# The expert stage of a five-stage kernel: blocks of 288 tokens with both layers' weights stationary

## The reference

```python
probs = softmax(ln(t) @ gate_w.T)          # 8 experts
top_v, top_i = top_k(probs, 2)
for e in range(8):
    h = silu(ln(t) @ w1[e] + b1[e])        # 512 -> 2048
    y = h @ w2[e] + b2[e]                  # 2048 -> 512
    out += y * comb_w[..., e:e+1]          # zero where e is not among the token's two
```

## Time and profile before

| what | value |
|---|---|
| three runs | 1467.91, 1471.44, 1472.68 us, median 1471.44 |
| the profiled execution | span 1469.3 us, mean granted clock 0.912 |
| expert stage, ahead of the loop | 931.5 to 986.05 us |
| its loop | 986.05 us to the last matmul at 1455.25 us |
| after the last matmul | to 1469.3 us |
| PE / DVE / ACT / POOL busy | 84% / 69% / 52% / 20% of the span |

### The profile page before, as it was taken

One profiled execution on the slowest core, in us unless ns is written; L12 is line 12 of the kernel. 1 busy time (PEld: TensorE's weight loads), 2 busy tenths in 40 slices (PEclk: granted clock), 3 DMA queues, 4 the chain that ended last, 5 costly groups with the idle time before them and its releaser, 6 DMA issues.

```text
span 1469.3 us, 33539 instructions
## 1 busy us (share of the span) xinstructions
PE 1237.3 (84%) x12366; PEld 848.8 (58%) x12367; DVE 1016.8 (69%) x1663; ACT 761.8 (52%) x1227; POOL 298.5 (20%) x363
## 2 busy tenths in 40 slices
PE   3735799998588999847489999768999999999996
PEld 2205576775466677423345555636677677767674
DVE  3668888888788888869567667475567755476432
ACT  2236577677666767622643424424466655375331
POOL 0121223332222333422000000034111111111111
PEclk9766999999899999979599999658999999999998
DMA  4043000003200000320220000328347564446111
GB/s 147 1 155 123 13 5 5 5 3 115 69 12 6 5 4 4 104 119 11 97 115 0 0 0 0 134 107 254 136 143 250 191 201 136 143 168 219 24 26 22
DMA packets 38129, 120.26 MB, mean 82 GB/s; under 512 B 9960, under 2 KB 14184, under 8 KB 28080
## 3 DMA queue, kind: packets, MB, share of 16 engines
q1 hardware_dynamic: 32416, 107.28, 20.3%
q0 software_dynamic: 5648, 12.13, 4.1%
HBM read 105.61 MB, written 12.76 MB: 81 GB/s over the span
## 4 chain that ended last, share of the span: by engine, by line
PE 47%; DVE 4%; ACT 2%; issue 2%; POOL 0%; POOLq 0%; DVEq 0%; ACTq 0%
PE banks L2349 16%; PE banks L2370 15%; PE banks L1880 7%; PE banks L1910 3%; PE banks L2319 1%; PE banks L2302 1%; PE banks L1936 1%; PE banks L2336 1%; PE banks L1949 1%; ACT ab_wi_hi L1749 1%; PE banks L2295 1%; PE banks L1959 1%; DVE f_qa L1418 0%; PE banks L1933 0%; ACT ab_un L1783 0%
## 5 line engine op out<-in xcount | busy, mean ns | idle before, releaser
L2349 PE MATMUL banks<-eb_x_hi,eb_w_hi 128*128 128x128 f16 x1344 | 228.7, 220 | 4.7 <-DVE eb_w_lo L2229 4.7
L2349 PE MATMUL banks<-eb_x_lo,eb_w_hi 128*128 128x128 f16 x1344 | 228.6, 220 | 0.0
L2349 PE MATMUL banks<-eb_x_hi,eb_w_lo 128*128 128x128 f16 x1344 | 228.6, 220 | 0.0
L1118 PE MATMUL banks<-mb_u_hi,mb_wi_hi 128*128 (+3 forms) x1088 | 190.7, 221 | 12.4 <-ACT mb_ca L845 10.7
L1118 PE MATMUL banks<-mb_u_hi,mb_wi_lo 128*128 (+3 forms) x1088 | 190.4, 221 | 0.0
L1118 PE MATMUL banks<-mb_u_lo,mb_wi_hi 128*128 (+3 forms) x1088 | 190.2, 221 | 0.0
L2229 DVE TENSOR_TENSOR eb_w_lo<-eb_raw,eb_w_hi 128x2048 f32 (+1 forms) x64 | 142.6, 2287 | 23.0 <-ACT eb_w_hi L2235 16.0
L647 DVE SCALAR_TENSOR_TENSOR mb_ca<-mb_xp,mb_par,mb_ca 128x128 f32<-128x128 f32 x384 | 149.5, 451 | 5.2 <-ACT mb_ca L845 3.4
L2349 PEld LDWEIGHTS banks<-eb_x_hi,eb_w_hi 128*128 128x128 f16 x1344 | 132.4, 99 | 7.4 <-issue 5.1
L2349 PEld LDWEIGHTS banks<-eb_x_lo,eb_w_hi 128*128 128x128 f16 x1344 | 132.4, 98 | 2.4
L2349 PEld LDWEIGHTS banks<-eb_x_hi,eb_w_lo 128*128 128x128 f16 x1344 | 132.4, 99 | 0.0
(11 more groups left out here) (441 smaller groups left out, 2842.6 us busy)
## 6 DMA issues: line engine op xcount, KB each, us to landing
eb_raw<-e_w SPq DMA_DIRECT2D x64, 1024.0 KB, 6.0
mb_ring<-m_in_w SPq DMA_DIRECT2D x8, 1072.0 KB, 6.5
ab_raw<-a_in_w SPq DMA_DIRECT2D x4, 1154.0 KB, 9.0
mb_ring<-m_out_w SPq DMA_DIRECT2D x4, 1024.0 KB, 5.3
xcm<-x_cm SPq DMA_DIRECT2D x4, 512.0 KB, 5.1
t_res<-x_tm SPq DMA_DIRECT2D x1, 2048.0 KB, 8.9
t_kept<-t_res SPq DMA_DIRECT2D x8, 256.0 KB, 2.0
mb_wi_hi<-t_kept SPq DMA_DIRECT2D x1, 2048.0 KB, 9.2
```

What stands on the lines that cost most here:

```text
L1118: x = e.matmul(ps[0:width, bank, n * P:(n + 1) * P], a[:, k, f:f + width], b[:, k, ds(i * P, P)], start=(k == 0 and m == 0), stop=(k == KD ...
L2349: o = e.matmul(ps[:, j, c * P:(c + 1) * P], a[:, side, k, f * P:(f + 1) * P], b[:, k, :], start=(k == 0 and m == 0), stop=(k == KD - 1 and ...
```

## The change: what it does, and the diff

Every expert gets one static block of 288 tokens (`CAP`), in three groups of rows, 128, 128 and 32. Unfilled places gather one of 384 spare rows and are added to spare rows of `out`. An expert with more than 288 tokens would have the rest done afterwards in a general loop (`overflows`, up to seven passes with an If on each engine).

Both layers hold a 128x128 piece of weights and stream the 288 tokens: 192 matmuls of 288 columns per layer and expert. `b1` and `b2` are the biases of the two activations; the mix of `b2` ahead of the loop, the slot table and its DMAs are gone. Layer 2 gives its result transposed, so the 288 results are transposed again (`turn_y`) before they are scaled and added to `out`.

The 8 x 16 steps of the main part are written out on each engine without a loop. In step s PE does layer 1 of piece s+3 (12 matmuls), in some steps an extra (f is the step within the expert): f=1 `listing` (24 matmuls of 3 columns that give the next expert's token numbers and mixing weights), f=2,3,4 `turn_y` of the last expert, f=9,10,11 `turn_x` of the next; then layer 2 of piece s (12 matmuls). ACT does two silus of 288 columns (float32 and the high part), the cast of one half piece of weights, and extras. DVE does the low part of the hidden values, the low part of a half piece, and extras: f=0 eight comparisons of 384 places (`mark`), f=1 `list_rows`, and so on. Weights come in half pieces of 128 x 1024, in six buffers, nine half pieces ahead. The gate's matmuls use float16 halves (12 of 8 columns per tile of tokens instead of 4 in float32).

```diff
+EX_PIECES = KD + EX_FB // 4
+EX_HALF = EX_F // 2
+EX_HALVES = [(k, 0) for k in range(KD)] + [(4, 0), (4, 1), (5, 0)] + [(k, 1) for k in range(KD)] + \
+    [(5, 1), (6, 0), (6, 1), (7, 0), (7, 1)]
+EX_N = len(EX_HALVES)
+EX_RAWS = 6
+EX_LEAD = 9
...
+EX_AHEAD = 3
+CAP = 288
+ROWS = ((0, P), (P, P), (2 * P, CAP - 2 * P))
+WIDE = len(ROWS) * P
...
+    def overflows(e, body):
+        e.wait_ge(plan_done, 1)
+        n = e.value_load(plan[0:1, OVER:OVER + 1], min_val=0, max_val=OVER)
+        with e.Fori(0, OVER) as o:
+            with e.If(o < n):
+                x = e.value_load(plan[0:1, ds(o, 1)], min_val=0, max_val=E - 1)
+                body(o, x)
...
-        for m in range(EX_RAWS, EX_PIECES + EX_RAWS):
-            e.wait_ge(wlo_done, m - EX_RAWS + 1)
-            if m == EX_PIECES:
-                e.wait_ge(xg_in, 16)
-            load(e, m, m % EX_RAWS)
-        e.wait_ge(b2_done, TT)
-        e.wait_ge(xg_in, 2 * 16)
-        for i in range(TT):
-            e.dma_start(core.out[i * P:(i + 1) * P, :], t[:, i, :]).then_inc(t_sent, 16)
-        with e.Fori(EX_PIECES // EX_RAWS + 1, E * EX_PIECES // EX_RAWS) as i:
-            for q in range(EX_RAWS):
-                e.wait_ge(wlo_done, i * EX_RAWS + (q - EX_RAWS + 1))
-                load(e, i * EX_RAWS + q, q)
+        for m in range(EX_RAWS, E * EX_N):
+            e.wait_ge(m_.wlo, m - EX_RAWS + 1)
+            load(e, m)
+            if m == 2 * EX_RAWS:
+                for i in range(TT):
+                    e.dma_start(core.out[i * P:(i + 1) * P, :], t[:, i, :]).then_inc(t_sent, 16)
...
+        def lower(s_, n, count, side):
+            piece, h = EX_HALVES[n % EX_N]
+            e.wait_ge(s_.whi, count + 1)
+            e.tensor_tensor(w_lo[:, side, piece, columns(h)], raw[n % EX_RAWS], w_hi[:, side, piece, columns(h)], ALU.subtract)\
+                .then_inc(s_.wlo, 1)
...
+        def mark(s_, values):
+            for i in range(TT):
+                e.tensor_scalar(marks[:, i, :], place[:], values(i), None, ALU.is_equal).then_inc(s_.marked, 1)
+        def list_rows(s_, count, slot):
+            e.wait_ge(s_.listed, count + 1)
+            own(e.tensor_copy(found[:], ps[:, TR, 0:3 * len(ROWS)].rearrange("p (r c) -> p r c", r=len(ROWS))))
+            own(e.scalar_tensor_tensor(out=empty[:], in0=found[:, :, 0], scalar=0.0, in1=trash[:], op0=ALU.is_equal, op1=ALU.mult))
+            e.scalar_tensor_tensor(out=gates[:, slot, :], in0=found[:, :, 2], scalar=1.0 / GATE_STEP, in1=found[:, :, 1],
+                                   op0=ALU.mult, op1=ALU.add)
+            e.scalar_tensor_tensor(out=rows[:, slot, :], in0=found[:, :, 0], scalar=-1.0, in1=empty[:], op0=ALU.add, op1=ALU.add)\
+                .then_inc(s_.rows_done, 1)
...
+        def low(s_, count, f):
+            e.wait_ge(s_.silu, count + 1)
+            e.tensor_tensor(h_lo[:, f % 4, :], hf[:, f % 2, :], h_hi[:, f % 4, :], ALU.subtract).then_inc(s_.low, 1)
+        def scale(s_, count, r, slot):
+            n = ROWS[r][1]
+            e.wait_ge(s_.y_tr, count * len(ROWS) + (r + 1))
+            e.tensor_scalar(y[0:n, r, :], ps[0:n, TR, :], gates[0:n, slot, r:r + 1], None, ALU.mult).then_inc(s_.y_done, 1)
...
+        mark(m_, lambda i: pm[:, i, 0:1])
+        list_rows(m_, 0, 0)
+        for m in range(EARLY_LOWS, EX_LEAD):
+            lower_main(m)
+        for r in range(len(ROWS)):
+            lower_x(m_, 0, r, 0)
...
+        for c in range(E * EX_FB):
+            low(m_, c, c % EX_FB)
+            s = c - EX_AHEAD
+            if s < 0:
+                continue
+            if EX_LEAD + s < E * EX_N:
+                lower_main(EX_LEAD + s)
+            x, f = divmod(s, EX_FB)
+            if f == 0 and x + 1 < E:
+                mark(m_, lambda i: pm[:, i, x + 1:x + 2])
+            if f == 1 and x > 1:
+                for r in range(len(ROWS)):
+                    e.wait_ge(m_.y_out[r], 16 * (x - 1))
+            if f == 1 and x + 1 < E:
+                list_rows(m_, x + 1, (x + 1) % 3)
+            if f in (2, 3, 4) and x:
+                scale(m_, x - 1, f - 2, (x - 1) % 3)
+            if f == 6 and x == 0:
+                plans()
+            if f in (9, 10, 11) and x + 1 < E:
+                lower_x(m_, x + 1, f - 9, (x + 1) % 2)
...
+        def upper_main(m):
+            x = m // EX_N
+            if x >= 2:
+                if EX_HALVES[m % EX_N][0] < KD:
+                    e.wait_ge(m_.h_mm, EX_FB * (x - 1))
+                else:
+                    e.wait_ge(m_.y_mm, KD * (x - 1))
+            upper(m_, m, m, x % 2, raw_in[m % EX_RAWS], 16 * (m // EX_RAWS + 1))
...
+        def silu(s_, count, f, bias):
+            e.wait_ge(s_.h_mm, count + 1)
+            e.activation(hf[:, f % 2, :], ps[:, 4 + f % 3, 0:CAP], ACT.Silu, bias=bias)
+            e.activation(h_hi[:, f % 4, :], ps[:, 4 + f % 3, 0:CAP], ACT.Silu, bias=bias).then_inc(s_.silu, 1)
+        def evacuate(s_, count, bias):
+            for d in range(KD):
+                e.wait_ge(s_.y_mm, count * KD + (d + 1))
+                e.activation(yb[:, d, :], ps[:, d, 0:CAP], ACT.Identity, bias=bias(d)).then_inc(s_.yb_done, 1)
...
+        for c in range(E * EX_FB):
+            x, f = divmod(c, EX_FB)
+            if c >= 2:
+                e.wait_ge(m_.low, c - 1)
+            silu(m_, c, c, b1[:, x, f:f + 1])
+            s = c - EX_AHEAD
+            if s < 0:
+                continue
+            if EX_LEAD + s < E * EX_N:
+                upper_main(EX_LEAD + s)
+            x, f = divmod(s, EX_FB)
+            if f in (9, 10, 11) and x + 1 < E:
+                upper_x(m_, x + 1, f - 9, (x + 1) % 2)
+            if f == EX_FB - 1:
+                if x:
+                    e.wait_ge(m_.y_tr, len(ROWS) * x)
+                else:
+                    e.wait_ge(t_sent, 16 * TT)
+                evacuate(m_, x, lambda d: b2[:, x, d:d + 1])
...
+        def listing(s_, marked, columns_of):
+            for r in range(len(ROWS)):
+                for i in range(TT):
+                    if r == 0:
+                        e.wait_ge(s_.marked, marked + (i + 1))
+                    x = e.matmul(ps[:, TR, 3 * r:3 * r + 3], marks[:, i, r * P:(r + 1) * P], columns_of(i),
+                                 start=(i == 0), stop=(i == TT - 1))
+            x.then_inc(s_.listed, 1)
+        def turn_x(s_, count, r):
+            n = ROWS[r][1]
+            e.wait_ge(s_.xg_in[r], count * 16 + 16)
+            if r:
+                e.wait_ge(s_.xlo, count * len(ROWS) + r)
             core.apart(e)
             for k in range(KD):
-                x = e.transpose(ps[:, 4, k * P:(k + 1) * P], xg[:, k * P:(k + 1) * P], core.ident[:])
...
+                x = e.transpose(ps[:, TR, k * P:k * P + n], xg[0:n, r, k * P:(k + 1) * P], core.ident[0:n, 0:n])
+            x.then_inc(s_.turned, 1)
...
+        def layer1(s_, f, side, xb, free):
+            if free is not None:
+                e.wait_ge(s_.silu, free)
+            for k in range(KD):
+                for n, (a, b) in enumerate(((w_hi, x_hi), (w_lo, x_hi), (w_hi, x_lo))):
+                    x = e.matmul(ps[:, 4 + f % 3, 0:CAP], a[:, side, k, f % EX_FB * P:(f % EX_FB + 1) * P], b[:, xb, k, :],
+                                 start=(k == 0 and n == 0), stop=(k == KD - 1 and n == 2))
+            x.then_inc(s_.h_mm, 1)
+        def layer2(s_, f, count, side, free=None):
+            e.wait_ge(s_.low, count + 1)
+            fx = f % EX_FB
+            at = fx % 4 * D
+            for d in range(KD):
+                if free is not None:
+                    e.wait_ge(s_.yb_done, free + (d + 1))
+                for n, (a, b) in enumerate(((w_hi, h_hi), (w_lo, h_hi), (w_hi, h_lo))):
+                    x = e.matmul(ps[:, d, 0:CAP], a[:, side, KD + fx // 4, at + d * P:at + (d + 1) * P], b[:, f % 4, :],
+                                 start=(fx == 0 and n == 0), stop=(fx == EX_FB - 1 and n == 2))
+                if fx == EX_FB - 1:
+                    x.then_inc(s_.y_mm, 1)
...
+        def layer1_main(c):
+            x, f = divmod(c, EX_FB)
+            if f == 0:
+                e.wait_ge(m_.xlo, len(ROWS) * (x + 1))
+                e.wait_ge(m_.wlo, x * EX_N + KD)
+            if f == EX_FB // 2:
+                e.wait_ge(m_.wlo, x * EX_N + EX_HALVES.index((KD - 1, 1)) + 1)
+            layer1(m_, c, x % 2, x % 2, c - 2 if c >= 3 else None)
+        e.wait_ge(tokg_done, 1)
+        listing(m_, 0, lambda i: tokg[:, i, 0, :])
+        for r in range(len(ROWS)):
+            turn_x(m_, 0, r)
+        for c in range(EX_AHEAD):
+            layer1_main(c)
+        for s in range(E * EX_FB):
+            x, f = divmod(s, EX_FB)
+            if s + EX_AHEAD < E * EX_FB:
+                layer1_main(s + EX_AHEAD)
+            if f == 1 and x + 1 < E:
+                listing(m_, TT * (x + 1), lambda i: tokg[:, i, x + 1, :])
+            if f in (2, 3, 4) and x:
+                if f == 2:
+                    e.wait_ge(m_.yb_done, KD * x)
```

(65 more changed lines are left out.)

537 lines of the change are left out of this document (263 added, 274 removed).

## The result

| | before | after |
|---|---|---|
| median of the runs (4 each) | 1469.9 us (1467.91 to 1472.68) | 1427.07 us (1426.08 to 1428.33) |
| profiled span | 1469.3 | 1425.4 |
| layer 1 of the first expert starts | 986.05 | 976.41 |
| last matmul ends | 1455.25 | 1410.66 |
| from there to the end of the span | 14.05 | 14.7 |

The ratio after/before is 0.970 (95%: 0.9682 to 0.9718). Of the span, 9.6 us went ahead of the loop and 34.95 in it (469.2 to 434.25), and 0.7 came back at the end. The forecast of 1436 us was 9 us too slow.

What follows compares the result with a forecast made beforehand. PE was taken to bound the kernel, busy 84% of the span. Ahead of the loop -12.4, loop -26.4 and end +3.0 gave a span of 1433.5 us; with 2.1 carried over, 1436 us, range 1410 to 1462.

Steps and rivals of the forecast that it cites:

- columns, 8 x 384 matmuls: Both layers on PE: 288-column matmuls 122.5 ns apart, 376.3 us in all for 442.7 before.
- 14 groups of turns without waits: PE's transposes of tokens and results in the loop: 0.44 + 0.44 + about 0.15 us per group, 14.4 in all.
- listing waits: PE waits at listings for DVE's marks: 3.5 us six times and 2.9 once, 24 us, between 0 and 35.
- clock behind them: PE's granted clock falls after each listing wait: 1.7 us each, 12 in all, between 0 and 16.
- waits at second turns: Second turn of each group waits for DVE's extra behind a low part: 14 x 0.6 = 8.4 us, between 0 and 17.
- last matmul to the end: After the loop: evacuation, turn, scale, three scatters and landing take 17 us, 3 more than before, between +1 and +8.
- the schedule from L: One step timed from L, a layer 1 piece's end: low part L+3.3, marks L+6.1, 0.6 later for six, listing L+7.2.
- a late gather: Ahead of the loop: layer 1 starts 12.4 us earlier, at 973.6, but only 8 earlier if the gather is late.
- B: Rival: the seven skips of the general loop stall for instructions, 17.6 to 35 us less 6 covered; 1456 us, chance 0.12.
- C: Rival: ACT's and DVE's pieces run one after another and set every step, 3.76 us; 1533 us, chance 0.05.
- D: Rival: an expert over 288 tokens goes through the general loop, 47 us of matmuls and some 30 of weights; 1515, chance 0.01.
- A: Rival: the listing wait is cheap, marks come before PE needs them or the clock holds; 1400 to 1420 us, chance 0.17.

Runs made afterwards that it cites:

- 1: Kernel after, with DVE making the marks for the next listing five steps earlier (f=12 of the expert before): 1412.9 us, 0.9613.
- 2: Kernel after, with the marks in step f=0 made ahead of the half piece's low part on DVE: 1410.93 us, 0.9594.
- Experiment 3: Kernel after, with 30 unneeded matmuls of 128 columns on PE ahead of each listing of the main part: 1424.22 us, 0.9689.
- 7: Kernel after, with the general loop for experts over 288 tokens left out on all engines: 1430.09 us, 0.9726.
- 5: Kernel after, with the tokens stored to the output behind the 24th half piece's load instead of the 12th: 1428.5 us, 0.9706.
- 6: Kernel after, with the turns' extras on DVE and cast of tokens on ACT put ahead of the half piece's work: 1421.45 us, 0.9663.
- 9: Kernel before, with layer 1 written once and its weight buffer chosen by a register instead of two copies: 1541.02 us, 1.0484.
- number 10: Kernel after, with marks five steps early, extras ahead of the half pieces and the later token store together: 1401.4 us, 0.9533.

## Why the prediction was right, and where its sizes were off

The mechanism held step by step; 8.1 us of span separate forecast (1433.5) and trace (1425.4). Part of the nearness is luck: the loop's terms were 14.9 us too large and 6.3 too small, and layer 1 started 2.8 late.

| term | forecast | measured |
|---|---|---|
| start of layer 1 | 973.6 | 976.41 |
| columns, 8 x 384 matmuls | 122.5 ns each | 122.5 (12 in 1.47 us) |
| 14 groups of turns without waits | 14.4 | 14 x 1.33 = 18.6 |
| listings without waits | 5.0 | 7 x 0.61 = 4.3 |
| listing waits | 24 | 2.1 + 6 x 2.5 = 17.1 |
| clock behind them | 12 | 7.4 - 1.3 = 6.1 |
| waits at second turns | 8.4 | 7 x 0.80 + 7 x 0.70 = 10.5 |
| slow start | 2.7 | 1.3 |
| loop | 442.8 | 434.25 |
| last matmul to the end | 17 | 14.7 |

- **Columns: exact.** Three widths of before (128, 256 and 512 columns) lay on one line, and this term alone carries the sign. The Trainium skill (TensorE: Matmul & The Clock Gate, "Wait — 56ns, not 53.3ns?") gives the start-to-start time at 2.4 GHz as the columns by 2.4 GHz and about 2.5 ns. An estimate from it for 288 columns is 122.5 ns too, and the trace agrees (12 in 1.47 us).
- **Listing waits: right cause (1 and 2), 7 us too large.** Against the schedule from L, the low part ended at L+3.6 (forecast 3.9), the last mark at L+5.45 (6.7), the listing at L+6.1 (7.2). The eight marks took 1.85 us of the chain, not 2.8: I had added the DVE slope of a float32 subtraction (1.06 ns a column) to a mark of another kind. By busy time a mark of 384 columns takes 0.24 us (13.4 us for 56) and one of 256 took 0.21, a slope of (0.24 - 0.21)/128 = 0.2 ns, near my lower bound, free width.
- **Clock: 6 us too large.** It fell behind four of the seven listings only (1.3 to 1.7 us each), though their waits agree within 0.05 us but for the first. Experiment 3 shows that all of the 6.1 go when PE is kept busy. Which of seven equal waits is followed by a fall stays open: with the same listings the traces of numbers 7, 5 and 6 have three, five and six falls, in place of four. Behind the waits of 0.8 us and less in number 2 there is none. The slow start of 2.7 was no better known: it takes 1.3 to 1.5 us in four of these traces and 2.5 to 2.9 in five others with 288 columns.
- **Turns: 4 us too small.** I had scaled the third turn, 32 rows, to 0.15 us; it takes 0.44 for the results, whose four matmuls hold 32 columns but still stream 128, and 0.45 for the tokens, whose four are only 32 wide. Number 6 shows that the waits, 10.5 us, are the half piece's cast and low part ahead of them.
- **Start: 2.8 us late, "a late gather".** The gate was done at 951.8 (3.8 before, forecast 3.4), the row numbers at 960.7 (962.7), but the first gather took 9.32 us on the chain. The store doesn't hold it up (5). What is left in the queues is the loads of weights; that they do wasn't shown.
- **End: three scatters, as predicted, 2.3 us too large.** The last was issued 8.1 us behind the last matmul for 7.8, and 6.7 us followed it for 6.1 + about 4. These three terms of the forecast add up to 17.9, not to the 17 that it states.
- **Rivals.** B is out: the skips cost nothing measurable (7), and what stalled in the kernel before were the first passes through its two copies (9). The Trainium skill (Runtime: NRT & Kernel Launch, Instruction fetch mechanics) says that a taken branch out of the current two pages waits for its target's load: the loads are there (four behind 1410 us, none in number 7), but no time shows a wait, and it could hide beside the landing. C is out: the steps without extras are 2.94 us long, PE's. D is out: 8 x 384 wide matmuls ran, and none of a general loop. A had a part of the truth, as the marks and the clock were cheaper than forecast.

What the change left on the table: 1.7% by the order of work, on DVE and ACT above all (number 10 against after, 0.9533 for 0.970), and 3.1% with 272 tokens, which is enough for these inputs.

## What to carry to other kernels

When a restructured stage turns all its stationary work into steps of one length, follow the in-order engines beside it through one step: a rare extra that PE needs at once belongs ahead of the bulk work of that step, or a whole round earlier. And a narrower block pays nearly in full only once those waits are gone (13.2 of 20.5 us of span with them, 17.7 without). For the price of an instruction, take a row of the same operation and type, also for its slope.

## What was not expected of the hardware

- A weight address from a register costs layer 1 of the kernel before 14.48 for 10.72 us, 20 ns a matmul on average, and only from about the 52nd matmul of a block on. Why it starts there wasn't tried.
- Eight float16 marks of 384 columns keep DVE busy for 1.9 us in a row, against 1.7 for eight of 256.
- An indirect gather lands in 7.6 us with five loads of 512 KB and the store around it, and in 7.8 without the store; the loads themselves take 7.0 and 7.4 there, and 3.8 as a median of the whole stage.
- Seven waits of 2.1 to 2.5 us, equal in what PE does, were followed by a granted clock of 0.50 four times and not at all three times.
- Seven skips of a general loop brought four instruction loads behind 1410 us and no time that can be measured.
